# Weight magnitudes of a transformer layer summed by ScalarE from a second layout, and a reordered tail

## The reference

```python
def bitnet_linear(x, weight, scale_param):
    s = jnp.maximum(jnp.mean(jnp.abs(weight), axis=1), 1e-08)
    binary_w = jnp.sign(weight / s[:, None])
    y = jnp.einsum('bsi,oi->bso', x, binary_w)
    y = y * (s * scale_param)[None, None, :]
    return jnp.nan_to_num(y, nan=0.0, posinf=1000000.0, neginf=-1000000.0)
...
x = L0_attn_hidden_states
xn = _layernorm(x, axis=-1)
x = x + _L0_attn_ref(xn, ...) + _L0_ffn_ref(xn, ...)   # 32 query heads of 16, 8 key heads; silu(gate) * up, then down
```

## Time and profile before

| | |
|---|---|
| median of 3 runs | 518.95 us (518.05 to 519.51) |
| the profiled execution | 519.96 us, of which 518.2 us from first to last instruction |
| TensorE busy | 493.8 us (95%) |
| VectorE busy | 418.3 us (81%) |
| ScalarE busy | 351.1 us (68%) |
| GpSimd busy | 97.4 us (19%) |
| the chain that ended last | PE 83%, ACT 7%, DVE 4%, DMA 3% |
| HBM traffic | 30.62 MB read, 10.35 MB written |

### The profile page before, as it was taken

How to read it: one execution, slowest core, us unless ns; L and a number is a source line. 1 busy time by engine, 2 the same in 40 slices (tenths; PEclk the granted TensorE clock), 3 DMA queues, 4 the chain that set the end, 5 groups by cost and what they waited for, 6 DMA issues and landing times.

```text
span 518.2 us, 9807 instructions
## 1 busy us (share of the span) xinstructions
PE 493.8 (95%) x3928; PEld 170.9 (33%) x3928; DVE 418.3 (81%) x483; ACT 351.1 (68%) x639; POOL 97.4 (19%) x140
## 2 busy tenths in 40 slices
PE   2899999999999999999999999999999999999995
PEld 1866444433432222222222222222222222223442
DVE  7459866876678999999999999999999942224795
ACT  2373545222337999999999999999999986774000
POOL 4200424744424000000000000000000121241031
PEclk9999999999999999999999999999999999999999
DMA  8901482443100911202102120110210214451321
GB/s 278 214 2 59 119 198 44 102 79 43 22 1 7 165 34 42 60 23 61 40 25 59 40 60 23 53 47 24 61 40 23 66 44 114 95 170 48 98 82 40
DMA packets 29956, 36.37 MB, mean 70 GB/s; under 512 B 6544, under 2 KB 20752, under 8 KB 29912
## 3 DMA queue, kind: packets, MB, share of 16 engines
q1 hardware_dynamic: 20888, 24.72, 16.0%
q0 software_dynamic: 8304, 10.95, 11.1%
q10 hardware_dynamic: 720, 0.08, 0.1%
HBM read 30.62 MB, written 10.35 MB: 79 GB/s over the span
## 4 chain that ended last, share of the span: by engine, by line
PE 83%; ACT 7%; DVE 4%; DMA 3%; issue 2%; SPq 1%; ACTq 0%; DVEq 0%
PE ps L1200 23%; PE ps L1072 19%; PE ps L1165 14%; PE ps L1133 9%; PE ps L1081 8%; ACT room L663 5%; PE ps L1051 3%; PE ps L1226 3%; DVE nmx L796 3%; PE ps L1004 2%; DMA room<-wq 2%; ACT osb L674 1%; DMA ga<-r_scratch 1%; PE ps L1043 1%; SPq L384 1%
## 5 line engine op out<-in xcount | busy, mean ns | idle before, releaser
L796 DVE TENSOR_REDUCE nmx<-ps 128x1 f32<-128x1024 f32 x256 | 293.3, 1213 | 9.9 <-PE ps L1081 9.7
L663 ACT ACTIVATE room<-ps 128x512 f32<-128x512 f32 x512 | 274.2, 597 | 21.3 <-PE ps L1165 11.2
L1200 PE MATMUL ps<-room,vcur 128*32 128x256 f32 (+1 forms) x1912 | 160.0, 406 | 4.4 <-ACT osb L674 4.2
L1165 PE MATMUL ps<-qst,kB 50*128 50x512 f16 x512 | 150.2, 383 | 2.5 <-ACT room L663 1.8
L1081 PE MATMUL ps<-kA,qst 48*128 48x512 f16 x512 | 145.3, 382 | 0.0
L1072 PE MATMUL ps<-room,wf 128*128 128x512 f16 x448 | 101.5, 381 | 0.0
L1200 PEld LDWEIGHTS ps<-room,vcur 128*32 128x32 f32 x1912 | 37.7, 108 | 99.9 <-issue 52.7
L1165 PEld LDWEIGHTS ps<-qst,kB 50*128 50x128 f16 x512 | 30.9, 93 | 114.5 <-ACT room L663 101.5
L644 ACT ACTIVATE room<-ps,gsc 128x512 f32<-128x512 f32 x28 | 19.2, 686 | 63.6 <-PE ps L1072 63.6
L1072 PEld LDWEIGHTS ps<-room,wf 128*128 128x128 f16 x448 | 42.5, 98 | 55.4 <-issue 8.0
L502 POOL TENSOR_TENSOR hlo<-room,hhi 128x512 f16<-128x512 f32 x28 | 34.1, 1216 | 98.2 <-ACT hhi L576 98.2
(11 more groups left out here) (128 smaller groups left out, 289.2 us busy)
## 6 DMA issues: line engine op xcount, KB each, us to landing
qst<-q_scratch SPq DMA_DIRECT2D x32, 192.0 KB, 3.4
o_scratch<-osb SPq DMA_DIRECT2D x16, 256.0 KB, 2.3
q_scratch<-parts SPq DMA_DIRECT2D x12, 256.0 KB
hlo<-x SPq DMA_DIRECT2D x8, 256.0 KB, 4.7
parts<-x POOLq DMA_DIRECT2D x8, 256.0 KB, 2.9
wf<-gate POOLq DMA_DIRECT2D x14, 128.0 KB, 3.7
wf<-up POOLq DMA_DIRECT2D x14, 128.0 KB, 4.0
wd<-down POOLq DMA_DIRECT2D x1, 1792.0 KB, 13.7
```

The lines of the kernel that those rows point to most:

```text
L663: nc.scalar.activation(probs[:, s % 2, r, :], ps[:, score_bank(entry(j, i)), :], ACT.Exp, scale=gam_reg[par][r]).then_inc(scores_free, 1)
L796: nc.vector.tensor_reduce(nmx[:, hf, idx:idx + 1], bank_pair(idx % 2), AX.X, ALU.max, negate=True).then_inc(rows_free, 1)
L1165: nc.tensor.matmul(ps[:, score_bank(e), :], kB[low:low + SROWS, par, kt % (TT // 2) * P:(kt % (TT // 2) + 1) * P], qst[low:low + SROWS, pa ...
L1200: mm = nc.tensor.matmul(ps[32 * r:32 * r + 32, 7, of], vcur[:, par, key_tile(r, j), :], probs[:, s % 2, r, of], start=(j == 0 and part == ...
```

## The change

- Each of the four attention weights is also passed in its natural layout (outputs on partitions): `wq_rows`, `wk_rows`, `wv_rows`, `wo_rows`. SP loads them into `natural` (the space of `absolute`) right behind the transposed ones, and waits for the last of them, instead of for `wv`, before it loads `wo`. GpSimd's feed-forward loads 1 to 3 wait for it too.
- ScalarE takes the magnitudes in six instructions (B0 to B5), each 128 x 512 with the sum along the row as a second output into `mag`. For the output weights it is four instructions (Y0) into `mago`. These rows are loaded over `wot`, after the sign W0 has been taken; SP waits for that inside its list, between the loads of the first heads and the stores of query tile 1. W0 moves from behind C5 to behind F9.
- The query and key factors stay on their partitions. The value and output factors are needed along the row: VectorE multiplies the identity with them (`vdiag`, and D1 into `ga`), and TensorE spreads each with one matmul by ones. The 40 and 8 recorded matmuls of the sums and GpSimd's additions go.
- The three hand-written orders are new. P0 and P1 now stand ahead of S0, Z0, U0.
- In the tail D7 is last instead of O7, C1 stands behind O2, and for the last tile GpSimd adds the input to the attention row.

```diff
     K_, V_ = "k", "v"
     PROJ = [K_, 0, V_] + list(range(1, QT))
-    pe_order = ("K0 X0 X1 X2 X3 K1 S0 X4 X5 G0 X6 Z0 X7 U0 P0 Z1 P1 Z2 G1 P2 U1 F2 F3 P3 F4 P4 F5 P5 F6 F7 A0 F8 F9 "
-                "A1 A2 F10 F11 A3 A4 F12 A5 A6 F13 A7 S1 F14 A8 A9 F15 A10 A11 F16 A12 A13 F17 A14 A15 F18 A16 F19 "
...
-    dve_order = ("M0 M1 J0 M2 M3 H0 M4 R0 N0 J1 N1 M5 N2 N3 M6 M7 H1 L0 R1 L1 N4 N5 L2 L3 S0 Z0 N6 N7 J2 L4 V0 L5 L6 "
...
-    act_order = ("D0 B0 C0 B1 B2 D1 C1 C2 N2 C3 C4 C5 W0 C6 N0 C7 F0 N1 E0 E1 X0 F1 F2 X1 Y0 F3 E3 F4 V2 E4 F5 X3 F6 "
-                 "E5 F7 F8 F9 X4 X5 F10 F11 F12 F13 F14 F15 F16 F17 F18 F19 F20 T0 F21 F22 F23 F24 F25 F26 F27 ")
+    pe_order = ("K0 K1 X0 X1 X2 X3 X4 X5 X6 X7 G0 P0 P1 S0 Z0 U0 Z1 G1 P2 Z2 P3 U1 F2 F3 F4 P4 P5 F5 F6 A0 F7 A1 A2 "
+                "F8 A3 A4 F9 A5 F10 F11 F12 A6 A7 F13 S1 F14 A8 A9 F15 A10 A11 F16 A12 A13 F17 A14 A15 F18 A16 F19 "
...
+    dve_order = ("M0 M1 J0 M2 J1 M3 H0 M4 R0 M5 N0 N1 M6 M7 L0 H1 N2 R1 N3 N4 L1 N5 L2 N6 N7 L3 L4 L5 L6 L7 J2 S0 Z0 "
+                 "g0 V0 Z1 G0 F0 Z2 g1 X0 Z3 G1 E2 F1 X1 g2 F2 G2 F3 g3 G3 X3 F4 g4 F5 G4 A0 F6 F7 A1 A2 A3 F8 A4 F9 "
+                 "g5 G5 F10 X4 F11 A5 X5 D1 A6 F12 A7 S1 F13 A8 A9 F14 A10 F15 A11 F16 A12 A13 A14 F17 A15 F18 F19 "
...
+    act_order = ("D0 C0 C1 D1 N1 C2 N2 C3 N0 C4 B5 C5 C6 C7 B4 B2 B0 B1 B3 F0 E0 E1 F1 X0 X1 F2 E3 F3 V2 X3 F4 E4 E5 "
+                 "F5 F6 X4 F7 F8 F9 W0 F10 X5 F11 Y0 F12 F13 F14 F15 F16 F17 F18 F19 F20 T0 F21 F22 F23 F24 F25 F26 "
...
-    tail = "O0 C0 O1 C1 O2 C2 O3 D4 D5 O4 O5 D6 O6 D7 O7"
+    tail = "O0 C0 O1 O2 C1 C2 O3 D4 D5 O4 O5 D6 O6 O7 D7"
...
-            sp.wait_ge(wv_loaded, 16)
+            sp.dma_start(natural[:, QT, :], wk_rows).then_inc(rows_k_loaded, 16)
+            sp.dma_start(natural[:, QT + 1, :], wv_rows).then_inc(rows_v_loaded, 16)
+            sp.dma_start(natural[:, 0:QT, :], wq_rows.rearrange("(t p) c -> p t c", p=P)).then_inc(rows_q_loaded, 16)
+            sp.wait_ge(rows_q_loaded, 16)
             sp.dma_start(wot[:, :, :], wo.rearrange("(c p) o -> p c o", p=P)).then_inc(wo_loaded, 16)
...
                                 load_queries(g, g, hf)
+                        sp.wait_ge(sign_wo_ready, 1)
+                        sp.dma_start(wot[:, :, :], wo_rows.rearrange("(t p) c -> p t c", p=P)).then_inc(rows_o_loaded, 16)
...
-                pool.wait_ge(ff_ready, i + 1)
+                to = ffn[i]
+                if i == TT - 1:
+                    to = att[:, i % 2, :]
+                    pool.wait_ge(att_ready, 2 * i + 2)
+                else:
+                    pool.wait_ge(ff_ready, i + 1)
...
-                    loaded, c0, nc_ = weights[n]
-                    act.wait_ge(loaded, 16)
-                    nc.scalar.activation(absolute[:, :, c0:c0 + nc_], wt[:, :, c0:c0 + nc_], ACT.Abs).then_inc(abs_ready, 1)
+                    t = [QT, *range(QT), QT + 1][n]
+                    act.wait_ge(rows_k_loaded if t == QT else rows_v_loaded if t > QT else rows_q_loaded, 16)
+                    nc.scalar.activation(natural[:, t, :], natural[:, t, :], ACT.Abs, accum_out=mag[:, t:t + 1]).then_inc(abs_ready, 1)
...
-                    act.wait_ge(sign_wo_ready, 1)
-                    nc.scalar.activation(wot, wot, ACT.Abs).then_inc(abs_wo_ready, 1)
+                    act.wait_ge(rows_o_loaded, 16)
+                    for t in range(HC):
+                        nc.scalar.activation(wot[:, t, :], wot[:, t, :], ACT.Abs,
+                                             accum_out=mago[:, t:t + 1]).then_inc(abs_wo_ready, 1)
...
-                    for col in range(QT + 1):
-                        for c in range(HC):
-                            nc.tensor.matmul(ps[:, 7, col:col + 1], absolute[:, c, col * P:(col + 1) * P], ones[:, 0:1],
-                                             start=(c == 0), stop=(c == HC - 1))
-                    for c in range(HC):
-                        mm = nc.tensor.matmul(ps[:, 7, KV:2 * KV], ones[:, :], absolute[:, c, NH * D + KV:NQKV],
-                                              start=(c == 0), stop=(c == HC - 1))
+                    pe.wait_ge(diag_v_ready, 1)
+                    mm = nc.tensor.matmul(ps[:, 7, KV:2 * KV], ones[:, :], vdiag[:, :], start=True, stop=True)
```

More of the change, by code:

```diff
@@ L25, with layer_kernel @@
 LIFT = 16384.0
-def layer_kernel(nc, x, wq, wk, wv, wo, sq, sk, sv, so, gate, up, down, sg, su, sd, out,
+def layer_kernel(nc, x, wq, wk, wv, wo, wq_rows, wk_rows, wv_rows, wo_rows, sq, sk, sv, so, gate, up, down, sg, su, sd, out,
                  q_scratch, k_scratch, o_scratch, r_scratch):
@@ L96, in layer_kernel @@
     D_OUT = [20, 24, 28]
-    tail = "O0 C0 O1 C1 O2 C2 O3 D4 D5 O4 O5 D6 O6 D7 O7"
+    tail = "O0 C0 O1 O2 C1 C2 O3 D4 D5 O4 O5 D6 O6 O7 D7"
+    assert tail.split()[-2:] == [f"O{TT - 1}", f"D{TT - 1}"]
     tail = [(step[0], int(step[1:])) for step in tail.split()]
@@ L178, in layer_kernel @@
         cqk = sb("cqk", [P, QT + 1], F32)
+        mag = sb("mag", [P, QT + 2], F32)
+        mago = sb("mago", [P, HC], F32)
         svb = sb("svb", [P, KV], F32)
+        vdiag = sb("vdiag", [P, P], F32)
         sob = sb("sob", [P, H], F32)
@@ L201, in layer_kernel @@
         qst = sb("qst", [P, 2, 2, REP, HALF], F16)
-        absolute = qst[:, :, :, :, :].rearrange("p a b h n -> p (a b h n)").bitcast(F32)[:, 0:HC * NQKV]
-        absolute = absolute.rearrange("p (c n) -> p c n", c=HC)
+        natural = qst[:, :, :, :, :].rearrange("p a b h n -> p (a b h n)").bitcast(F32)[:, 0:(QT + 2) * H]
+        natural = natural.rearrange("p (t c) -> p t c", c=H)
         kA = sb("kA", [P, 2, HALF], F16)
@@ L251, in layer_kernel @@
         abs_wo_ready = sem("abs_wo_ready")
-        mag_step = sem("mag_step")
-        mag_ready = sem("mag_ready")
+        diag_v_ready = sem("diag_v_ready")
+        diag_o_ready = sem("diag_o_ready")
+        rows_q_loaded = sem("rows_q_loaded")
+        rows_k_loaded = sem("rows_k_loaded")
+        rows_v_loaded = sem("rows_v_loaded")
+        rows_o_loaded = sem("rows_o_loaded")
         sums_ready = sem("sums_ready")
@@ L812, in _ @@
                     hidden_factors(n)
+                elif kind == "D":
+                    dve.wait_ge(abs_wo_ready, HC)
+                    step(nc.vector.tensor_scalar(mago[:, :], mago[:, :], 1.0 / H, SMALL, ALU.mult, ALU.max))
+                    for t in range(HC):
+                        nc.vector.tensor_scalar(ga[:, t * P:(t + 1) * P], ident[:, :], mago[:, t:t + 1], None,
+                                                ALU.mult).then_inc(diag_o_ready, 1)
                 elif kind == "E" and PROJ[n] == V_:
@@ L821, in _ @@
                 elif kind == "S" and n == 0:
-                    dve.wait_ge(sums_ready, 1)
+                    dve.wait_ge(abs_ready, QT + 2)
                     dve.wait_ge(vec_loaded, 16 * 3)
[L825 to L828, removed]
+                    step(nc.vector.tensor_scalar(mag[:, :], mag[:, :], 1.0 / H, SMALL, ALU.mult, ALU.max))
+                    nc.vector.tensor_tensor(cqk[:, :], mag[:, 0:QT + 1], scqk[:, :], ALU.mult).then_inc(factors_ready, 1)
+                    nc.vector.tensor_scalar(vdiag[:, :], ident[:, :], mag[:, QT + 1:QT + 2], None, ALU.mult).then_inc(diag_v_ready, 1)
+                    dve.wait_ge(factors_ready, 1)
                 elif kind == "Z" and n == 0:
@@ L861, in _ @@
                     dve.wait_ge(sums_ready, 2)
[L862 removed]
                     dve.wait_ge(sob_loaded, 16)
[L864 to L865 removed]
+                    nc.vector.scalar_tensor_tensor(out=sob[:, :], in0=sob[:, :], scalar=vg[:, 2:3],
+                                                   in1=ps[:, 2 * (SUM_AT % 2), :], op0=ALU.mult,
+                                                   op1=ALU.mult).then_inc(factors_ready, 1)
                     dve.wait_ge(dsb_loaded, 16)
@@ L894, in _ @@
                 elif kind == "V":
+                    dve.wait_ge(sums_ready, 1)
+                    dve.wait_ge(both_ready, 1)
+                    nc.vector.tensor_tensor(svb[:, :], ps[:, 7, KV:2 * KV], svb[:, :], ALU.mult).then_inc(factors_ready, 1)
                     dve.wait_ge(factors_ready, 2)
@@ L945, in rows_out, with sum_out @@
                 guard(att[:, i % 2, :], H).then_inc(att_ready, 1)
-                dve.wait_ge(att_ready, 2 * i + 2)
+                if i < TT - 1:
+                    dve.wait_ge(att_ready, 2 * i + 2)
+                    sum_out(i)
+            def sum_out(i):
                 dve.wait_ge(res_added, i + 1)
+                dve.wait_ge(ff_ready, i + 1)
                 nc.vector.tensor_tensor(ffn[i], ffn[i], att[:, i % 2, :], ALU.add).then_inc(out_ready, 1)
@@ L1236, in _ @@
                             down_proj(i, f, part)
-_INS = ["x", "wq", "wk", "wv", "wo", "sq", "sk", "sv", "so", "gate", "up", "down", "sg", "su", "sd"]
+_INS = ["x", "wq", "wk", "wv", "wo", "wq_rows", "wk_rows", "wv_rows", "wo_rows", "sq", "sk", "sv", "so", "gate", "up", "down", "sg", "su", "sd"]
```

(4 more changed lines are left out.)

28 lines of the change are left out of this document (9 added, 19 removed), and 4 rows, old and new, of the table dve_order.

## The result

The changed kernel takes 514.72 us (median of 7 runs) against 520.26 for the kernel before in the same runs: ratio 0.9893, 95% interval 0.9868 to 0.9918, so 1.1% or about 5.5 us faster. I had predicted 6.2 us less. The profiled execution takes 514.21 us (before 519.96). The sum came out close, but two of its terms were far off and two costs or gains were missing from it; they happened to cancel.

What follows compares the result with a forecast made beforehand. TensorE was taken as the bound. Gains of 6.4 us (start) and 2.15 (tail) less 2.4 (store wait) made 6.2 us, so 512.8 us from a median of 518.95; range 509.3 to 516.3.

Steps and rivals of the forecast that it cites:

- The start: Start of the kernel on TensorE: removing the magnitude sums was to put it 6.4 us earlier, first projection at 24.4 us.
- I take 25.6: At the start: TensorE's clock rises at 25.6 us, 4.5 us after G0's start at 21.1; the first projection loses 0.6 us.
- rival (a): At the start: clock rises early, at 21 us, as transpositions count; 2.4 us more gained, 510.4 us. Chance 0.2.
- Rival (d): At the start: narrow magnitude matmuls prepared the clock; without them it stays at 1.2 GHz, kernel slower, e.g. 522.5 us. Chance 0.05.
- My sentence that the trace agreed with it: At the start: eight transpositions at 26.8 to 28.5 us, all slow, agree with the skill that transposes do not raise the clock.
- The new wait: In the middle: SP's wait and 1 MB load before query tile stores 1 to 3 delay TensorE at A7; 2.4 us lost.
- the middle of 1.2 and 3.9: TensorE's wait before A7: 1.2 us with stores alone, 3.9 with 2.7 us for the 1 MB load; 2.4 taken.
- The attention stage is not touched: Attention stage, 160 to 470 us: the change was said not to touch it, predicted difference 0.
- The tail: End of the kernel: with D7 last, 1.45 instead of 3.6 us from TensorE's end to VectorE's; 2.15 us gained.
- The six row sums: On ScalarE at the start: 0.55 to 1.2 us each, cost nothing; cover 0.9 us at the worst bound.
- VectorE's new small steps: At the start: VectorE's S0, V0 and extra diagonals, about 0.3 us each, fit in its waits of 1 to 4 us.
- (b): In the middle: store wait at its bound, 3.9 instead of 2.4 us, 514.3 us; 516.3 with late clock rise. Chance 0.2.

Runs made afterwards that it cites:

- the normalization edit alone: Kernel before with only the last attention block's output normalization and split steps one step later: 517.22 us (median of 4), 0.9923 of the kernel before.

## Why the prediction was right in its sum and not in its terms

- **The start: right in kind, too small.** VectorE's chain is what holds P0 back, as worked out (its last low part ends at 21.8 us against my 22.4). The failing step is "I take 25.6" for the rise of the clock. It rose near 18 us, even before rival (a)'s 21 (the transpositions ran unbroken from 14.6, not 16.4), so G0 took 1.9 us instead of 3.4 and P0 lost nothing; another 0.8 us is G0's start at 20.04 instead of 20.9. Together TensorE is 9.3 us ahead instead of 6.4. I had read the long busy stretch of the earlier trace rows as one that fails to raise the level although it is busy, and asked when something else would raise it. The two runs with narrow matmuls show what it was: put ahead of the transpositions they leave those behind them at the low level, and put behind the rise they are the only thing on TensorE while the level falls. Removing them removed their 8.7 us and the slow time behind them. Rival (d) had it upside down.
- **The Trainium skill's rule** ("TensorE: Matmul & The Clock Gate", Part 4) that transposes do not count for the clock is contradicted by the changed kernel: the level rose behind fp32 transpositions and three tiny matmuls only. (The page's durations there are of bf16 transposes, of which no run here has one.) My sentence that the trace agreed with it rested on the eight slow ones at 26.8 to 28.5 us, which came after 8.7 us of narrow matmuls.
- **The granted clock** of 1.00 in the earlier trace rows was no evidence either way: in the traces of both kernels it reads 1.00 in stretches that have the durations of the low level (432 ns in 14 to 17 us after). In the trace with the normalization edit alone the same sums read 0.50:

```profile
18.20:28.00 9.80, 9.80 (x47) 9.80 (x48) 3.79 (x13) 1.40 (x3) 0.55 (x2) 0.50 0.87 196
```

- **The new wait: the mechanism right, its size not.** Place, chain (SP's wait, tile 1's stores, X5, F11, A5, A7) and the price with stores alone (1.2 against 1.10 us) held. The step that failed is "the middle of 1.2 and 3.9", and its upper end with it: the load in flight adds 4.1 us and not 2.7 at most. I had divided its 1 MB by the 392 GB/s of the earlier trace rows; from the load's issue to X5 the DMA engines moved 195 GB/s (last number; before it their busy share). Why it is so little no run shows. The measured stop is 5.62 us.

```profile
80.40:92.10 11.70, 9.80 (x46) 4.21 (x44) 6.42 (x9) 1.20 (x3) 2.28 (x3) 1.00 0.69 195
```

- **Left out: the clock behind a stop.** I priced a stop at its length. The 5.6 us stop brought the level down and cost another 2.0 us, 1.6 of them in the sixteen matmuls behind it. In the five other traces with this stop (5.4 to 5.7 us) the sixteen take 5.27 to 6.36 us instead of 3.63, so this price varies from 1.6 to 2.7 us.
- **Left out: the normalization steps.** One line of the diff, two lists of numbers, worth 2.3 us in the traces of the two kernels. "The attention stage is not touched" was a step that I had not checked against the diff.
- **The tail** came out as worked: 2.1 us for 2.15. GpSimd's addition ended at 508.09 and the scaling at 508.85, so the cover was 0.8 us, more than I gave it.
- **The six row sums and VectorE's new small steps** cost nothing, as said.

In gain against the prediction that is +2.9 (start), -5.2 (stop and clock, 7.6 against 2.4), +2.3 (steps) and -0.5 (end of the span): -0.5 in all, which explains the 514.21 us of the profiled execution against my 513.8. That is luck. The chances hid it: rivals (a) and (b) had 0.2 each and none for both, and what happened is (a) together with a loss of 7.6 us in the middle, well beyond (b)'s 3.9.

## What to carry to other kernels

When a queue's list gets a new wait, price everything that stands behind it on that queue, and measure transfers under the load that they will meet, not alone; moving one wait and its load behind three stores was worth more (about 6.7 us, 508.05 against 514.72, each beside the kernel before at 520.1 to 520.3) than the whole change. Price a long stop of TensorE at its length and the stretch at half rate behind it: every trace here with a stop of 5.4 to 8.5 us in this stage has one. Before a stage is called untouched, read every line of the diff for it, lists of step numbers most of all.

## What the runs showed of the hardware

- The granted clock fell from 1.00 over 0.68 to 0.50 (2.4 to 1.2 GHz) in three successive stretches in which TensorE was fully busy with one-column fp32 matmuls. It rose within a run of fp32 transpositions (432, 354, 284 ns).
- The rise came between about 17.5 and 20.6 us in six traces with the same start: one trace gives its moment to 2 or 3 us at best.
- The granted clock fell behind a stop of 1.54 us in one trace (0.62 over 4.5 us) and did not behind one of 1.22 us in another (the fp16 matmuls behind it stay at 0.38 us).
- Three stores of 256 KB from the first issue to the waiting engine: 7.0 and 7.2 us with no 1 MB load in flight (the kernel before, for the key, and the run with the load held back), 11.25 with a 1 MB load in flight on the same queue and 11.5 on another.
- An activation with a sum along the row is followed by a read of the accumulator of 0.19 us; from the start of one to the start of the next it is 0.62 us for 128x512.
